# A graph kernel of two stages on one core: TensorE's counts for the other engines come from a drain behind a step's last matmul

## The reference, cut to what matters

```python
# layer 0, x: 3125 x 64
h1, h2, h3, h4 = node_proj(x, W1..W4, b1..b4, node_type)
w5e   = edge_feat @ W5[edge_type] + b5[edge_type]            # 16 features
num   = sum(h3[dst] * (h4[src] + w5e))
score = softmax((num / 4)[:, None], axis=-1)[:, 0]           # over an axis of length one
out   = h1 + segment_sum(score * (h2[src] + w5e), dst)
x     = layernorm(x + out)
# layer 1
m     = relu(x[src] + edge_feats @ We + be) + 1e-7           # 32 features
ez    = exp(m - segment_max(m, dst)[dst])
agg   = segment_sum(m * ez / segment_sum(ez, dst)[dst], dst)
x     = layernorm(x + (x + agg) @ Wm + bm)
```

## Time and profile before

| | |
|---|---|
| runs | 2187.74, 2188.85, 2201.08 us, median 2188.85 |
| span of the profiled execution, first to last instruction | 2193.7 us |
| PE busy | 1808.2 us (82%), 9,200 matmuls |
| DVE busy | 1649.8 us (75%) |
| ACT busy | 791.6 us (36%) |
| POOL busy | 1282.8 us (58%) |

### The profile page before, as it was taken

One profiled execution on the slowest core, in us unless ns is written; L12 is line 12 of the kernel. 1 busy time (PEld: TensorE's weight loads), 2 busy tenths in 40 slices (PEclk: granted clock), 3 DMA queues, 4 the chain that ended last, 5 costly groups with the idle time before them and its releaser, 6 DMA issues.

```text
span 2193.7 us, 29535 instructions
## 1 busy us (share of the span) xinstructions
PE 1808.2 (82%) x9200; PEld 1086.3 (50%) x9200; DVE 1649.8 (75%) x3316; ACT 791.6 (36%) x1503; POOL 1282.8 (58%) x1347
## 2 busy tenths in 40 slices
PE   6599999999999999999981678788887878879863
PEld 5334555655555655555560245445444544545432
DVE  6534877878878788788787378778887877878876
ACT  3101223223322333223231145455554545545561
POOL 7365666666666666666614666666666666666624
PEclk9899999999999999999995789889998998989975
DMA  8933445554545555555442245555554545555541
GB/s 283 391 61 94 139 144 148 148 151 144 148 142 153 143 146 145 147 148 152 138 141 58 48 134 156 141 151 157 153 149 142 164 140 162 149 149 153 151 140 57
DMA packets 216065, 321.30 MB, mean 146 GB/s; under 512 B 61931, under 2 KB 123940, under 8 KB 215781
## 3 DMA queue, kind: packets, MB, share of 16 engines
q1 hardware_dynamic: 128950, 148.58, 23.3%
q0 software_dynamic: 43056, 68.05, 13.8%
q10 hardware_dynamic: 43904, 102.79, 13.1%
HBM read 186.00 MB, written 133.22 MB: 146 GB/s over the span
## 4 chain that ended last, share of the span: by engine, by line
PE 29%; issue 26%; DVE 16%; another core or an unknown queue 12%; ACT 11%; ACTq 3%; POOL 1%; DMA 1%; SPq 0%; DVEq 0%; POOLq 0%
PE wide L900 11%; PE wide L999 7%; DVE late L1210 3%; ACT block L819 3%; DVE edge_lists L1210 3%; DVE featm L1226 2%; DVE score L1216 2%; ACTq L812 2%; ACT prob_wide L796 2%; PE wide L1010 2%; ACT msg L797 1%; DVE h3d L1235 1%; ACT block L800 1%; PE wide L860 1%
## 5 line engine op out<-in xcount | busy, mean ns | idle before, releaser
L634 POOL DMA_INDIRECT rows<-d_x,idx x588 | 558.3, 950 | 342.1 <-issue 158.2
L624 POOL DMA_INDIRECT block<-d_h,idx x482 | 455.6, 945 | 278.8 <-issue 126.2
L900 PE MATMUL wide<-late,typed 125*128 125x512 bf16 (+1 forms) x936 | 282.4, 382 | 35.7 <-issue 35.3
L999 PE MATMUL wide<-late,ntype_i 125*128 125x512 bf16 x975 | 239.5, 403 | 53.9 <-DVE ntype_i L1346 49.7
L900 PE MATMUL wide<-edge_lists,typed 125*128 125x512 bf16 (+1 forms) x864 | 259.8, 381 | 22.1 <-issue 20.9
L1235 DVE TENSOR_TENSOR_SCAN h3d<-keep,h3d,bank 128x512 f32<-128x512 bf16 x98 | 125.4, 1280 | 176.4 <-issue 171.2
L999 PE MATMUL wide<-edge_lists,ntype_i 125*128 125x512 bf16 x936 | 223.4, 393 | 11.1 <-issue 11.0
L624 POOL DMA_INDIRECT rows<-d_h,idx x160 | 151.0, 944 | 132.7 <-remote 48.4
L1010 PE MATMUL wide<-ident,block 128*128 128x128 f32 x784 | 135.3, 319 | 93.6 <-ACT block L819 59.3
L999 PEld LDWEIGHTS wide<-late,ntype_i 125*128 125x128 bf16 x975 | 100.9, 104 | 175.9 <-DVE ntype_i L1346 50.1
L900 PE MATMUL wide<-late,ntype_i 125*128 125x512 bf16 (+1 forms) x468 | 179.0, 383 | 3.9 <-issue 3.5
(11 more groups left out here) (224 smaller groups left out, 3390.0 us busy)
## 6 DMA issues: line engine op xcount, KB each, us to landing
d_run<-block ACTq DMA_DIRECT2D x98, 512.0 KB
d_inj<-zeros SPq DMA_DIRECT2D x28, 896.0 KB
inj<-d_inj SPq DMA_DIRECT2D x98, 256.0 KB
d_run<-stage ACTq DMA_DIRECT2D x98, 256.0 KB
feat<-in_ea16x3T SPq DMA_DIRECT2D x196, 96.0 KB
types<-d_type SPq DMA_DIRECT2D x196, 64.0 KB
keep<-d_keep SPq DMA_DIRECT2D x196, 64.0 KB
keep<-d_pen SPq DMA_DIRECT2D x196, 64.0 KB
```

Of the source, the lines that this page charges most:

```text
L624: pool.indirect_dma_start(out=ring[c % RING][:, j, h, :], out_offset=None, in_=d_h24, in_offset=bass.IndirectOffsetOnAxis(ap=idx[:, c, at: ...
L634: pool.indirect_dma_start(out=rows1[c % RING1][:, j, h, :], out_offset=None, in_=d_x1, in_offset=bass.IndirectOffsetOnAxis(ap=idx[:, c, at ...
L900: ins = pe.matmul(p_pick[s][:, 0:cols], table0[n][:, k, :], hot0[b][:, k - b * KT, 0:cols], start=(k == 0 and n == 0), stop=(k == NT - 1 a ...
L999: ins = pe.matmul(p_hot[s], table[q][:, SPLIT * k:SPLIT * (k + 1), :].rearrange("p b c -> p (b c)"), hot[s][:, k, :], start=(k == 0 and q ...
```

## The change

In seven places the count is no longer raised by the last matmul of the step. A drain instruction of TensorE follows that matmul, and the drain raises the count. The matmuls, their order, the waits, the counts and all that the other engines do stay as they are. The steps `numerator` and `turn_run`, and what comes before and behind the two loops, are not changed.

```diff
@@ pick0
                     if k in (KT - 1, NT - 1):
-                        ins.then_inc(picked[b], 1)
+                        pe.drain().then_inc(picked[b], 1)
@@ turn_inj
-                ins.then_inc(injT[s], 1)
+                pe.drain().then_inc(injT[s], 1)
@@ difference
-                add_rows(s, c, 0).then_inc(q2_ready[s], 1)
+                add_rows(s, c, 0)
+                pe.drain().then_inc(q2_ready[s], 1)
@@ turn_prob
-                ins.then_inc(probT[s], 1)
+                pe.drain().then_inc(probT[s], 1)
@@ project1
-                ins.then_inc(z_ready[s], 1)
+                pe.drain().then_inc(z_ready[s], 1)
@@ pick
                 if half:
-                    ins.then_inc(picked[s], 1)
+                    pe.drain().then_inc(picked[s], 1)
@@ turn1
-                ins.then_inc(turned[s], 1)
+                pe.drain().then_inc(turned[s], 1)
```

## The result

Three runs of the changed kernel took 2374.56, 2378.36 and 2379.96 us, median 2378.36. The ratio to the kernel before is 1.0847, 95% interval 1.0805 to 1.0889. The forecast was 2130 us. The profiled execution has a span of 2372.7 us, 179.0 more than before.

What follows compares the result with a forecast made beforehand. TensorE was taken to bound stage 0, and late counts (holds) to lengthen stage 1. Span 2193.7 + 25 (stage 0) - 8 (ahead of the loop) - 76 (stage 1) = 2134.7, less 4.85: 2130 us; range 2030 to 2390.

Steps and rivals of the forecast that it cites:

- first rival: Both stages: holds stay and drains come on top, 107 us in stage 0, 88 in stage 1, total 2387; chance 0.28.
- The price of a drain: One drain in TensorE's matmul stream: 0.32 us, 0.37 where the next step waits for two counts; bounds 0.21 to 0.60.
- the second wait: Where the next step waits for two counts, a separate wait of 0.051 us, until now taken ahead, becomes exposed.
- the rest of the sum (tail, end, restart, slow first matmuls): Each drain: 0.16 us tail, 0.05 drain's end, 0.05 restart, 0.06 slower first matmuls, together 0.32 us.
- Half of `probT`: Stage 0: of this drain's 0.32 us only half was counted, since TensorE often stands there anyway.
- the 8.93 us: Stage 0: TensorE's own need per chunk, 3.75 us plus 5.18 us of picks, out of 9.77 us.
- Stage 0: Drains add 1.10 us a chunk, holds' end frees 0.84; period becomes 10.03 us, +25 us over 97 chunks.
- Stage 1: Holds go, drains add 0.91 us to 7.2; 8.3 us a chunk taken instead of 9.08, -76 us.
- Ahead of the loop: From 100 to 200 us: 11 us of TensorE's idle time won, less 10 drains of 0.32, -8 us.
- The sign I had given for being wrong: Drains of over 1 us in the middle of a stage would mean that they sit out the hold.
- The rival with the cheap drain: Holds go and a drain costs 0.21 us: stage 0 9.50 us, stage 1 7.73 a chunk, 2021 us; chance 0.14.

Runs made afterwards that it cites:

- e4: Changed kernel's seven places, but counts raised by the last matmul and a drain that raises nothing behind it: 2367 us, ratio 1.0791 to the kernel before.
- e5: Changed kernel with all drains, but one indirect DMA a chunk instead of 6 or 8 after each stage's first chunks, other rows left out: 2142 us, ratio 0.9705.
- e6: Kernel before, counts by matmuls, with gathers thinned to one indirect DMA a chunk, other rows left out: 1928 us, ratio 0.8736.
- e8: Changed kernel, but in stage 0 GpSimd starts a chunk's gathers at a later `injT` instead of `q2_ready`; nothing left out: 2388 us, ratio 1.0808.
- e11: Kernel before with drains only for `picked` and `turned` in stage 1, all other counts by matmuls: 2205 us, ratio 0.9986.
- e12: Kernel before with drains only for `q2_ready` and `probT` in stage 0: 2258 us, ratio 1.023.
- e7: Changed kernel with all 6 or 8 indirect DMAs a chunk, but only 8 bytes of each row fetched after the first chunks: 2419 us, ratio 1.0958.
- e13: Changed kernel with all 6 or 8 indirect DMAs a chunk, full rows, but only 16 of 128 rows each after the first chunks: 2461 us, ratio 1.1228.
- e9: Changed kernel with few gathers, each left-out indirect DMA replaced by a GpSimd memset of 128 x 1024 bf16: 2207 us, ratio 0.9994 to the kernel before.

## Why the prediction was wrong

**The step that failed** is in the first rival's "against": "a count is held where work is not, and a drain waits for work alone". The one drain in the trace of before stood at 2188.6, with no gather of GpSimd under way, so it said nothing on this. Count and drain both wait for TensorE's report, and that is what is late (e4). The row that would have shown it was in the trace. GpSimd in the hold of the earlier trace rows, which I read only for its restart:

```profile
1615.83 0.94 POOL L634 DMA_INDIRECT rows<-d_x,idx  x1 [0.30 <-issue]
1619.67 0.94 POOL L634 DMA_INDIRECT rows<-d_x,idx  x1 [2.90 <-remote]
```

The six gathers ended at 1616.77, the counts were seen 2.4 us after that. In the hold of the earlier trace rows the last one ended at 329.19, and L1235 started 2.05 us after that. I asked what TensorE did in a hold, and not what ended just ahead of its end.

**The price of a drain** was sized about right, 0.37 us predicted with two waits behind it and 0.32 with one. Where it isn't held, start to start over a drain takes 0.51 us in place of 0.11 with two waits behind it (0.40), and 0.35 in place of 0.11 or 0.46 in place of 0.22 with one (0.24). So the second wait costs 0.16 us where I had 0.05, and the rest of the sum (tail, end, restart, slow first matmuls) was 0.08 too high. No run measures those four one by one. Where hardly a hold is left the price alone makes the change a loss: e5 takes 214 us more than e6, 0.35 us a drain. The Trainium skill (PSUM — Partial Sum Buffer, Engine vs sequencer instructions) keeps the increment on the matmul and the drain for a barrier. As to the cost of going against that, a drain takes 0.24 to 0.40 us here where nothing else delays it. The Trainium skill also says in that section that the matmul's update fires on its completion; here it was seen up to 3.4 us after the modelled end in e4 and up to 6.1 in the kernel before, and 0.01 us after it for each `z_ready` of e6 but the first.

**Half of `probT`** was too little. The sum starts from the 8.93 us in which TensorE never stands, and there the drain costs its whole 0.24 us: L900 starts at least 0.35 us behind the last L947 in each of the 93 chunks where it follows. Against the kernel before, where TensorE often stood at this place, nothing was lost (38.8 us from L946 to L900 over 93 chunks, 35.6 after).

**Stage 0** was to take 10.03 us. With few gathers it takes 10.35 (e5), 0.32 more. With the measured prices the drains are 1.19 us a chunk and not 1.10; on e6's 8.99 and with 0.10 of late ends in e5's first chunks that gives 10.28. In the changed kernel stage 0 takes 11.63: the late ends of 97 us are 1.00 us a chunk, 0.90 more than e5's, and 0.38 stay unassigned (the lower clock behind a hold, 0.95 over the stage, may be part of it). **Stage 1** was to take 8.3 us; without holds 7.81, with them 8.99. The late ends between its first and last scan are 103 us, 1.06 a chunk: 7.81 + 1.06 = 8.87, and 0.12 stay unassigned. There the holds had cost the kernel before as much already (9.08 against 7.05 in e6), so the drains changed little, where I had a gain of 76 us and the rival a loss of 88. **Ahead of the loop** I had -8 and it was +8: three drains of `picked` at 104.8, 149.1 and 183.9 ended 6.6 to 7.6 us late.

The forecast's 2130 us lies near e5's 2142, but by luck: by e5's periods stage 0 was 31 us over it, what lies ahead of stage 0 22 over, stage 1 48 under. And that is no gain of the change, since the kernel before with the same few gathers takes 1928 us. The forecast had the drains end the holds; in these runs only fewer or paused gathers shortened them. The first rival named the mechanism. Its total (2387) is near by luck: 107 us in stage 0 were 180, 88 in stage 1 were -9. The sign I had given for being wrong, drains of over 1 us in mid-stage, came. The rival with the cheap drain has a slip: 0.21 us at the same places is 0.66 a chunk and not 0.57, which moves its 2021 us by 9.

## What to carry to other kernels

A drain makes its engine stand until its work is reported, so where reports come late it turns a late count, which others may not mind, into standing time of the busiest engine. Before you add or remove one, look for what ends just ahead of a late count, also on engines that have nothing to do with it. Here that is GpSimd's indirect DMAs, whose price isn't in their own rows (1928 us with few of them, 2189 with all). Cost the hold at every place to which it can move, since taking it off one drain put it on the next (e8, e11, e12). And price the drains as if there were no hold: here that alone was 214 us.

## What I had not expected of the hardware

- TensorE's reports (drain ends, counts by matmuls) are late while indirect DMAs of GpSimd are in flight, once a group has run for some 4 to 6 us, and mostly come 1.4 to 2.1 us after its last one. A group of eight holds them 2.6 us longer than one of six. It is so with 8-byte rows (e7) and with 16 rows (e13, there mostly 1.9 to 2.8 us after the last) as well. What all these have in common with the full gathers, and a memset lacks, isn't shown.
- A memset on GpSimd slows some of VectorE's work. Its one-hots of stage 1 (the same operation and shape, a row of e5 and one of e9) went from 359 to 556 ns, those of stage 0 from 356 to 520, while the f32 scan of stage 1 took 1281 ns in both. In stage 1 VectorE was busy 811 of 825 us in e9, after 687 of 758 in e5, so its 8.51 us a chunk are VectorE's; stage 0, which TensorE bounds, stayed at 10.35:

```profile
L1318 DVE TENSOR_SCALAR late<-zeros,slot_of 125x512 bf16<-125x512 f16 x325 | 93.6, 359 | 0.0
```
```profile
L1329 DVE TENSOR_SCALAR late<-zeros,slot_of 125x512 bf16<-125x512 f16 x325 | 158.9, 556 | 0.0
```

- After TensorE stood for 5.27 us in e8 its granted clock was at the lower level, 1.2 GHz (0.50 from 563.65 to 565.13, and 1.00 from 548 to 556, ahead of the hold), and the picks started every 0.43 us, where they take 0.216:

```profile
563.65 0.63 PE L901 MATMUL wide<-late,ntype_i 125*128 125x512 bf16 x1
...
564.07 1.06 PE L901 MATMUL wide<-late,typed 125*128 125x512 bf16 x2
```
